# Scores by key in two halves beside the scores by query, in the second cross attention of a six-stage kernel

## What is computed

```python
q = x @ Wq
xc = jnp.concatenate((mem, x), axis=1)
kv = xc @ Wkv
k, v = jnp.split(kv, 2, axis=-1)
q, k, v = (to_heads(q), to_heads(k), to_heads(v))
dots = jnp.einsum('bhid,bhjd->bhij', q, k) * scale
mask = j_idx > i_idx + mem_len
dots = jnp.where(mask[None, None], -jnp.inf, dots)
attn = jax.nn.softmax(dots, axis=-1)
out = jnp.einsum('bhij,bhjd->bhid', attn, v)
return out.transpose(0, 2, 1, 3).reshape(b, n, dim) @ Wout + bout
```

## Time and profile before

| | |
|---|---|
| time, median of 3 runs | 873.44 us (872.77 to 874.19) |
| profiled execution: time, span | 873.73 us, 871.9 us |
| TensorE busy | 785.4 us, 90% of the span |
| VectorE, ScalarE, POOL busy | 492.0, 404.9, 110.6 us |
| stage 4, about | 542 to 692 us of the span |

### The profile page before, as it was taken

The page is one execution under the profiler, slowest core; times in us unless marked ns, Lnnn a source line. Parts: engine busy times, 40 slices in busy tenths (PEclk is TensorE's granted clock), DMA queues, the critical chain, the costliest instruction groups (busy, mean ns, idle before and its releaser), DMA issues.

```text
span 871.9 us, 17126 instructions
## 1 busy us (share of the span) xinstructions
PE 785.4 (90%) x6680; PEld 396.7 (45%) x6681; DVE 492.0 (56%) x1166; ACT 404.9 (46%) x735; POOL 110.6 (13%) x107
## 2 busy tenths in 40 slices
PE   6999999997988869999986867899999899999996
PEld 4445354444555533433324444455656544443332
DVE  1543323324888876566448773365666466646662
ACT  3737354554566652333431332355545344554454
POOL 1270221211000000000003445121110000000000
PEclk9999999999899998999997998899999899999998
DMA  9400000000000000000000000000000000000000
GB/s 359 170 2 1 1 0 0 1 2 1 2 2 1 1 2 0 0 1 0 0 1 1 1 0 0 2 3 3 3 3 3 2 0 1 1 1 0 13 12 24
DMA packets 2372, 13.51 MB, mean 15 GB/s; under 512 B 256, under 2 KB 256, under 8 KB 1664
## 3 DMA queue, kind: packets, MB, share of 16 engines
q1 hardware_dynamic: 2304, 12.56, 3.6%
HBM read 11.51 MB, written 1.05 MB: 14 GB/s over the span
## 4 chain that ended last, share of the span: by engine, by line
PE 70%; DVE 13%; ACT 8%; issue 7%; DMA 1%; DVEq 0%; POOL 0%; ACTq 0%; SPq 0%
PE bank L1726 6%; PE bank L2097 4%; PE bank L2338 4%; PE bank L1952 3%; PE bank L2264 3%; PE bank L1764 3%; PE bank L2317 3%; PE bank L2274 3%; PE bank L1777 3%; PE bank L1968 3%; PE bank L1957 3%; PE bank L2116 2%; PE bank L2158 2%; PE bank L121 2%; DVE sb_rowmax L1099 2%
## 5 line engine op out<-in xcount | busy, mean ns | idle before, releaser
L1726 PE MATMUL bank<-sb_xT,sb_arena 128*128 128x512 f32 (+1 forms) x128 | 63.1, 626 | 3.5 <-ACT sb_arena L605 2.5
L1418 DVE TENSOR_REDUCE sb_rowmax<-bank 128x4 f32<-128x512 f32 x64 | 41.1, 684 | 33.8 <-PE bank L2104 33.1
L605 ACT ACTIVATE sb_arena<-bank 128x512 f32<-128x512 f32 x64 | 37.4, 597 | 37.6 <-PE bank L1726 37.5
L1030 DVE TENSOR_TENSOR sb_arena<-bank,sb_arena 128x512 f32<-128x512 f32 x32 | 22.1, 690 | 50.2 <-PE bank L1777 49.9
L757 ACT ACTIVATE sb_arena<-bank 128x512 f32<-128x512 f32 x36 | 21.4, 596 | 55.6 <-PE bank L1952 54.1
L513 POOL TENSOR_TENSOR sb_arena<-sb_la,sb_consts 128x1024 f32<-128x1024 f32 x16 | 30.6, 1920 | 112.2 <-PE bank L1764 88.8
L1952 PE MATMUL bank<-sb_xT,sb_w 128*128 128x512 f32 (+1 forms) x72 | 40.7, 648 | 0.0
L1726 PEld LDWEIGHTS bank<-sb_xT,sb_arena 128*128 128x128 f32 x128 | 22.4, 194 | 37.3 <-ACT sb_arena L605 21.9
L852 ACT ACTIVATE sb_arena<-bank 128x512 f32<-128x512 f32 x64 | 33.0, 605 | 13.3 <-PE bank L2130 13.3
L2097 PE MATMUL bank<-sb_arena 32*64 32x256 f32 x512 | 35.8, 395 | 3.0 <-ACT sb_arena L837 2.9
L1646 DVE TENSOR_TENSOR sb_arena<-sb_arena,bank 128x512 f32<-128x512 f32 x32 | 21.0, 683 | 29.7 <-PE bank L2321 22.0
(11 more groups left out here) (344 smaller groups left out, 1640.3 us busy)
## 6 DMA issues: line engine op xcount, KB each, us to landing
sb_w<-w SPq DMA_DIRECT2D x1, 2646.5 KB, 25.6
sb_consts<-consts SPq DMA_DIRECT2D x1, 1812.0 KB, 14.4
sb_w<-w SPq DMA_DIRECT2D x1, 1736.0 KB, 19.4
sb_w<-w SPq DMA_DIRECT2D x1, 1175.0 KB, 9.2
sb_arena<-w SPq DMA_DIRECT2D x2, 512.0 KB, 4.1
sb_ctxT<-ctx SPq DMA_DIRECT2D x1, 1024.0 KB, 16.4
out<-sb_xT SPq DMA_DIRECT2D x4, 256.0 KB, 2.5
sb_xT<-x SPq DMA_DIRECT2D x1, 768.0 KB, 10.6
```

Of the source, the lines that this page charges most:

```text
L605: act.activation(V[:, h, :], bank[h % 2][:], ACT.Copy).then_inc(s_vev, 1)
L1418: dve.tensor_reduce(rowmax4[k % 2][:, 4 * g:4 * g + 4], bank[n][:].rearrange("p (j t) -> p j t", j=4), AX, ALU.max).then_inc(s_mx4, 1)
L1726: pe.matmul(bank[h % 2][:], KT[:, h, :], cols(c), start=True, stop=True).then_inc(s_v, 1)
```

## The change

- `scores_by_key4` is gone as a function. Its matmuls and masks move into `scores4`, half by half: while half 0 of pair k works on groups 0 and 1 it also issues the scores by key of pair k - 1 for groups 2 and 3, and half 1 the other way around (`KEY_GROUPS` = 2, 3, 0, 1). In a half the order is: 4 matmuls by query, 2 by key, 4 by query, 2 by key, then 4 masks by key, then 8 masks by query. `scores4` is now called for i = 16 too, with scores by key alone.
- The waits of both stand at the head of `scores4`; of the exps of the pair before the last one, half 0 needs the first two and half 1 all.
- `exps4` and `less_max4` take the groups in the order of `KEY_GROUPS`.
- `k4` has three buffers of 4 sequences instead of two halves, and `k_copy4(h)` waits for pair 2h - 5 instead of 2h - 3.
- On ScalarE the square of the norm comes ahead of the exps in iterations 7, 11 and 15.

```diff
-    k4 = take(SEQS * P).rearrange("p (b t) -> p b t", b=SEQS)
+    k4 = [ap.rearrange("p (b t) -> p b t", b=4) for ap in (take(4 * P), take(4 * P), sb("k4_third", [P, 4 * P])[:])]
...
+    KEY_GROUPS = (2, 3, 0, 1)
...
         def k_copy4(h):
             wait(act, s_k4, h + 1)
-            wait(act, s_t4, 4 * (2 * h - 2))
-            act.activation(k4[:, half_rows(h), :], bank[4][:].rearrange("p (b t) -> p b t", b=4), ACT.Copy).then_inc(s_kx4, 1)
+            wait(act, s_t4, 4 * (2 * h - 4))
+            act.activation(k4[h % 3], bank[4][:].rearrange("p (b t) -> p b t", b=4), ACT.Copy).then_inc(s_kx4, 1)
...
+                if i in OUT_AT:
+                    tail4(OUT_AT[i], 1)
                 if 1 <= i <= PAIRS:
                     exps4(i - 1)
                 if i < PAIRS:
                     maxima_copy4(i)
-                if i in OUT_AT:
-                    tail4(OUT_AT[i], 1)
...
         def scores4(k, half):
-            groups = (2 * half, 2 * half + 1)
-            b0 = 2 * (k % 4)
-            wait(pe, s_kx4, 5 * (k // 2) + 5)
-            wait(pe, s_qc4, k // 2 + 1)
-            wait(pe, s_mx4, 4 * k + 2 * half)
+            groups, key_groups = (2 * half, 2 * half + 1), KEY_GROUPS[2 * half:2 * half + 2]
+            b0, e0 = 2 * (k % 4), 2 * ((k - 1) % 2)
+            if k < PAIRS:
+                wait(pe, s_kx4, 5 * (k // 2) + 5)
+                wait(pe, s_qc4, k // 2 + 1)
+                wait(pe, s_mx4, 4 * k + 2 * half)
+            if k > 0:
+                wait(pe, s_kx4, 5 * ((k - 1) // 2) + 1)
+                wait(pe, s_qx4, 4 * ((k - 1) // 2) + 4)
+                wait(pe, s_e4, 4 * (k - 1) - 2 + 2 * half)
             for part in range(2):
                 at = slice(SEQ * part, SEQ * part + SEQ)
+                if k < PAIRS:
+                    for g in groups:
+                        scored = bank[g % 2][:].rearrange("p (j t) -> p j t", j=4)
+                        for b in range(2):
+                            q = (b0 + b) * SEQ
+                            pe.matmul(scored[64 * b:64 * b + 64, :, at], q4[rows(g), q:q + SEQ], kx4[rows(g), b0 + b, :, at],
+                                      start=(part == 0), stop=True, skip_group_check=(part == 1))
+                if k > 0:
+                    for g in key_groups:
+                        pe.matmul(by_key[g][:, 256 * part:256 * part + 256], k4[(k - 1) // 2 % 3][rows(g), e0 + part, :],
+                                  qx4[rows(g), 2 * ((k - 1) % 4) + part].rearrange("p j q -> p (j q)"), start=(part == 0),
+                                  stop=True, skip_group_check=(part == 1))
+            if k > 0:
+                for h in range(2):
+                    for g in key_groups:
+                        o = 64 + 32 * h
+                        pe.matmul(by_key[g][o:o + 32, :].rearrange("p (a q) -> p a q", q=SEQ), eye32[rows(g)],
+                                  early_query[rows(g), h].unsqueeze(1).to_broadcast([32, 8, SEQ]), start=False, stop=True,
+                                  skip_group_check=True)
...
-        def scores_by_key4(k):
-            b0 = 2 * (k % 4)
-            wait(pe, s_kx4, 5 * (k // 2) + 1)
-            wait(pe, s_qx4, 4 * (k // 2) + 4)
-            wait(pe, s_e4, 4 * k)
...
             for i in range(PAIRS + 2):
-                if i < PAIRS:
+                if i <= PAIRS:
                     scores4(i, 0)
-                if 1 <= i <= PAIRS:
-                    scores_by_key4(i - 1)
-
...
-                if i < PAIRS:
+                if i <= PAIRS:
                     scores4(i, 1)
```

## The result

The changed kernel takes 913.7 us (911.02 to 917.23, 4 runs) against 873.82 us: ratio 1.045, 95% interval 1.041 to 1.050. I had said 895.5 us with a range of 884 to 907. The direction was right, the size was not.

A forecast was written before the change was run, and what follows sets the result against it. TensorE was taken to bound stage 4. Array +24.0, iteration 16 +1.2, third buffer -5.0 and added waits +1.9 gave +22.1 us on the profiled 873.73: 895.8, forecast 895.5 us as the median is 0.3 lower; range 884 to 907.

The forecast's parts named there:

- Emptying at a change of shape, and the price of a half: TensorE, stage 4 scores: each tile-shape change empties the array; a half takes 2.76 us, +24.0 us over 15 iterations.
- The witness with disjoint array rows at 600.63: Half 1, masks to less_max4: the next matmul shares no array rows or bank, yet starts 0.23 us later.
- Third buffer: Copy of projected keys (k4) ahead of pv4: all 6 TensorE stalls go, -5.0 us.
- Scores_by_key in i = 16, exps, square, POOL: Iteration 16 +1.2 us; waiting for exps nothing (cover 0.9 us); moving the norm's square free; POOL waits as before.
- Added waits: Scores by query, half 1, wait for row maxima at i = 3, 5 (0.3 us each) and 14 (1.3): +1.9 us.
- The clock: TensorE's granted clock in stage 4: no term in the sum, a lower clock appears only as a rival.
- the clock's rival: Stage 4: emptied array counts as less work, clock lowered, eight more spells, +12 us, 907.5 us; chance 7%.
- the first rival: Stage 4 scores: both tile shapes stream together, a half takes 1.36 us, -19.9 us in all, 853.5 us; chance 10%.

The follow-up runs named there:

- the kernel with one shape: The changed kernel with each 32 x 128 matmul by key cut into two of 32 x 64: 863.3 us, ratio 0.9897; measured again 865.6 us, 0.9935.
- the order turned round: The kernel with one shape, with the wait for the row maxima last and masks by query ahead of those by key: 863.3 us, ratio 0.9886.
- the kernel with half-filled rounds and the old waits: The kernel before, its scores by key issued as two separate groups, each with its masks and half the tiles per round, no wait moved: 900.6 us, ratio 1.032.

## Why the prediction failed, step by step

- **Emptying at a change of shape, and the price of a half**: right. Forecast 2.76 us, measured 2.76; +24.0 and +1.2 us stand. The witness with disjoint array rows at 600.63 carried it, and the kernel with one shape is the proof. The Trainium skill says in TensorEngine Tiling (Array Packing), Key Properties, that a change of tiling mode drains TensorE; the pieces of 0.59 and 0.63 us agree. The Trainium skill's TensorE: Matmul & The Clock Gate, Part 3, has small matmuls on different tiles of the array overlap; the half of 1.38 us agrees, within one shape.
- **Third buffer**: right, -5.0 forecast, -4.7 measured alone (-2.2 to -6.8).
- **Scores_by_key in i = 16, exps, square, POOL**: nothing of them shows up as late.
- **Added waits**: the term was +1.9 us and should have been 5.8. By the lengths of TensorE's groups: iterations 3 and 5 lose 0.7 us each, not 0.3 (602.35 to 604.15 = 1.80 instead of 1.09); iteration 14 loses 1.6, not 1.3; four even iterations 0.2 each, which I had called hidden by 0.06 us; and the transpose, also called hidden, 0.4 us in five of them. Two prices were too low. VectorE starts its maxima 0.51 us after the masks' start (602.03 to 602.54), not 0.38. And TensorE resumes 0.32 us after they end, not 0.1, because three more waits are queued behind the late one; with the order turned round it was 0.14.
- **The clock**: the step that failed. The sum held it constant; it cost about 15 us (+15.6 by the table, +14.4 at 0.46 us each), the largest miss. I had it as a rival, with the right mechanism's name and the wrong place and price: 12 us at 7%, argued away with "no gap over 0.2 us in most iterations". The row that should have warned me is rows 10: there the clock fell behind one wait of 1.5 us, in the iteration that the change makes thinner still, and that spell grew from 3.4 to 13.7 us. So the rival was right that half-filled rounds have a part in it, as the kernel with half-filled rounds and the old waits shows too (29.0 us of low clock against 15.5). How much each cause has of the 15 us stays open.
- **Together**: 25.2 (array) + 15.6 (clock) - 5.0 + 5.8 (waits) = 41.6 us; the profiled runs differ by 39.8 (873.73 and 913.53). With 14.4 us for the clock the sum is 40.4, within 1 us of the difference.
- **The range** ended at 907 because the clock's rival was cut off at its far end while one cause of it, the waits, was itself undersized. The two were not independent, and I treated them so.

## What to carry to other kernels

Small matmuls on different array rows run side by side only when their tiles have the same shape; cut the larger tile into the shape of the smaller and issue them alternately. In this kernel that brought the halves to half their length, but only 1 to 4 us of time beyond the third buffer. When a change takes away work that covered a wait on TensorE, price the wait with every wait instruction queued behind the late one, and then ask what the clock does behind it. A forecast for a TensorE-bound stage needs a term for the clock in its sum, not only among the rivals.

## What I had not expected of the hardware

- The low clock came behind a wait as short as 0.64 us (before 604.15), though not behind its twin before 584.39, and filling waits of 0.7 to 1.8 us with useless matmuls made the kernel 10.0 us faster. In stretches of half-filled rounds it also came with no wait of over 0.2 us ahead (at 624 us, and at 650 us in the kernel with half-filled rounds alone).
- Eight 32 x 64 tiles stream fp32 at once, in rounds of 0.22 us like four: sixteen records in flight at 577.41.
- Denser code has pauses of its own: 9 to 10 us in the kernel with one shape, ended by nothing that the profile's waits show. They are about as large as what lies between its 863 us and the 853.5 us of the first rival, which held waits of only 1.9 us and the clock as before.
